# TensorE adds the gathered source rows in PSUM by identity products, in place of VectorE's addition

## The reference, cut to what matters

```python
h_src = h[row]
ef = jnp.concatenate([h_src, h[col]], axis=1)
edge_weights = jax.nn.sigmoid(jax.nn.relu(ef @ We1 + be1) @ We2 + be2)[:, 0]
aggr = jax.ops.segment_sum(edge_weights[:, None] * h_src, col, num_segments=n)
gate = jax.nn.sigmoid(jnp.concatenate([h, aggr], axis=-1) @ Wg + bg)
h_new = gate * aggr + (1.0 - gate) * h
```

## Time and profile before

| | us |
|---|---|
| median of 3 runs | 2142.13 (2141.02 to 2144.42) |
| span of the profiled execution | 2383.5 |

### The profile page before, as it was taken

One profiled execution on the slowest core, in us unless ns is written; L12 is line 12 of the kernel. 1 busy time (PEld: TensorE's weight loads), 2 busy tenths in 40 slices (PEclk: granted clock), 3 DMA queues, 4 the chain that ended last, 5 costly groups with the idle time before them and its releaser, 6 DMA issues.

```text
span 2383.5 us, 40155 instructions
## 1 busy us (share of the span) xinstructions
PE 1765.2 (74%) x12318; PEld 1600.5 (67%) x12319; DVE 1849.8 (78%) x5049; ACT 1086.9 (46%) x2658; POOL 1410.9 (59%) x1430
## 2 busy tenths in 40 slices
PE   4999986725654577878877878878877788777790
PEld 3787875525554576767777777777777787777760
DVE  7788777738986688887888877888887777777766
ACT  2566655635531244443444444454444433444325
POOL 4555303763666666666666666666666666666635
PEclk9999996966665567576667665666676656666665
DMA  7899991353444455545454555555555555555401
GB/s 274 293 331 327 332 305 41 118 179 91 124 121 135 118 154 145 152 145 157 144 154 146 155 152 162 161 163 153 154 165 163 160 155 161 162 159 156 141 24 54
DMA packets 278498, 392.59 MB, mean 165 GB/s; under 512 B 74753, under 2 KB 178436, under 8 KB 278155
## 3 DMA queue, kind: packets, MB, share of 16 engines
q1 hardware_dynamic: 218783, 230.00, 30.7%
q0 software_dynamic: 57024, 155.79, 22.1%
q10 hardware_dynamic: 2476, 4.22, 0.5%
HBM read 374.69 MB, written 15.12 MB: 164 GB/s over the span
## 4 chain that ended last, share of the span: by engine, by line
PE 59%; DVE 17%; issue 16%; DVEq 4%; another core or an unknown queue 3%; ACT 1%; DMA 0%; SPq 0%; POOL 0%; ACTq 0%; POOLq 0%
PE psum L585 13%; PE psum L535 8%; PE psum L1467 7%; PE psum L1468 7%; PE psum L1489 6%; PE psum L564 4%; DVE sums L1913 3%; PE psum L1497 3%; DVE weighted L580 3%; DVE psum L574 2%; PE psum L1446 2%; PE psum L1354 2%; DVEq L1978 2%; DVE logit L576 1%
## 5 line engine op out<-in xcount | busy, mean ns | idle before, releaser
L981 POOL DMA_INDIRECT x_rows<-src_table,lane_src x720 | 692.9, 962 | 397.6 <-issue 193.6
L574 DVE SCALAR_TENSOR_TENSOR psum<-psum,we_all 128x1024 f32<-128x1024 f32 (+1 forms) x273 | 268.9, 985 | 191.4 <-remote 116.6
L1468 PE MATMUL psum<-ring,sums 128*128 128x128 f32 x980 | 285.1, 372 | 99.0 <-issue 97.8
L589 DVE TENSOR_TENSOR sums<-sums,psum 128x128 f32 (+4 forms) x812 | 200.9, 247 | 189.7 <-issue 117.3
L1467 PE MATMUL psum<-ring,sums 128*128 128x128 f32 x980 | 294.1, 387 | 68.0 <-issue 65.6
L981 POOL DMA_INDIRECT late_gathers<-src_table,lane_src x232 | 224.5, 968 | 134.9 <-issue 61.9
L981 POOL DMA_INDIRECT ring<-src_table,lane_src x236 | 226.9, 962 | 123.0 <-issue 63.4
L1468 PEld LDWEIGHTS psum<-ring,sums 128*128 128x128 f32 x980 | 231.6, 282 | 99.0 <-issue 98.3
L576 DVE TENSOR_REDUCE logit<-psum 128x8 f32<-128x1024 f32 (+1 forms) x273 | 266.9, 978 | 21.9 <-issue 2.1
L585 PE MATMUL psum<-weighted,x_rows 128*128 128x40 f32 x1440 | 265.0, 359 | 23.2 <-issue 23.2
L585 PEld LDWEIGHTS psum<-weighted,x_rows 128*128 128x128 f32 x1440 | 264.1, 281 | 22.5 <-issue 22.5
(11 more groups left out here) (263 smaller groups left out, 3680.4 us busy)
## 6 DMA issues: line engine op xcount, KB each, us to landing
ring<-in_edge_attr SPq DMA_DIRECT2D x195, 512.0 KB, 5.3
ring<-rel_table SPq DMA_DIRECT2D x74, 512.0 KB
ring<-cell_table SPq DMA_DIRECT2D x121, 256.0 KB
ring<-src_table SPq DMA_DIRECT2D x144, 128.0 KB
x_rows<-src_table,lane_src POOLq DMA_INDIRECT x720
ring<-dst_table SPq DMA_DIRECT2D x297, 32.0 KB
ring<-src_table SPq DMA_DIRECT2D x104, 64.0 KB
src_table<-ring SPq DMA_DIRECT2D x12, 512.0 KB, 2.9
```

What stands on the lines that cost most here:

```text
L574: eng.scalar_tensor_tensor(hid, hid, 0.0, wide["we2"][:, :].unsqueeze(1).to_broadcast([P, n, P]), ALU.max, ALU.mult)
L589: return eng.tensor_tensor(table[..., bass.ds(start, width)], table[..., bass.ds(start, width)], part, ALU.add)
L981: eng.indirect_dma_start(gathered(c)[:, j, :], None, src_table, bass.IndirectOffsetOnAxis(ap=lane_src[:, t:t + 1], axis=0)).then_inc(gathe ...
L1468: last = eng.matmul(o, node_hot[:, u % 2, 1, e], base_dst[:, k % 2, :], start=False, stop=True, skip_group_check=True)
```

## The change

`add_src_part` becomes four TensorE products per chunk with the f32 identity as stationary operand and the gathered source part as moving operand. They accumulate onto the destination part: in `dst_part` only the first of four products starts a group, and the new ones end it. A new stage `hidden_sum(q)` stands last in TensorE's turn, behind `rider_mm`; it now has the wait for the gathers. VectorE waits for `hidden_sum` where it waited for `hidden` and the gathers, and its addition and the drain behind it are gone. The buffers, the other waits and all work on ScalarE, GpSimd and the DMA queues stay. In the setup one wait is written in another way (`step(last)`). The body of `far` treats edges out of reach of a chunk's window in the same way.

```diff
         def dst_part(eng, out, hot_t, win):
             for j in range(J):
-                last = eng.matmul(out[:, j, :], hot_t[:, j, :], win, start=True, stop=True, skip_group_check=True)
+                last = eng.matmul(out[:, j, :], hot_t[:, j, :], win, start=(j == 0), stop=False, skip_group_check=True)
             return last
 
         def add_src_part(eng, out, rows_):
-            return eng.tensor_tensor(out, out, rows_[:, :, 0:P], ALU.add)
+            for j in range(J):
+                last = eng.matmul(out[:, j, :], ident[:, :], rows_[:, j, 0:P], start=False, stop=True, skip_group_check=True)
+            return last
...
-            run_stages(n_steps, [(1, hidden_mm), (4, wsum), (1, rider_mm)])
+            def hidden_sum(q):
+                for j in range(2):
+                    eng.wait_ge(gather_in[q % (G_SLOTS // 2)][j], 32 * sum(len(pair_chunks(i)) for i in range(q % (G_SLOTS // 2), q + 1, G_SLOTS // 2)))
+                for c in pair_chunks(q):
+                    last = add_src_part(eng, hidden(c), gathered(c))
+                last.then_inc(done("hidden_sum"), 1)
+
+            run_stages(n_steps, [(1, hidden_mm), (4, wsum), (1, rider_mm), (1, hidden_sum)])
...
-                need(eng, "hidden", q)
-                for j in range(2):
-                    eng.wait_ge(gather_in[q % (G_SLOTS // 2)][j], 32 * sum(len(pair_chunks(i)) for i in range(q % (G_SLOTS // 2), q + 1, G_SLOTS // 2)))
+                need(eng, "hidden_sum", q)
                 n = len(pair_chunks(q))
-                add_src_part(eng, hidden_pair(q), gathered_pair(q))
                 need(eng, "weight", q - 4)
-                eng.drain()
                 edge_dots(eng, logit[:, q % 4, 0:n, :].rearrange("p c j -> p (c j)"), hidden_pair(q)).then_inc(done("logit"), 1)
```

More of the change, by code:

```diff
@@ L267, in gnn_pair @@
         assert own_slots % 2 == 0 and G_SLOTS % 2 == 0
[L269 to L280, removed]
         spare = ring_slots[RING_GATHERS]
@@ L1517, in far @@
                 eng.wait_ge(done("far_window"), item * 16)
-                dst_part(eng, hidden(0), onehot3_t[:, 0, 0, :, :], window[0:WP, 0, :]).then_inc(done("far_hidden"), 1)
+                dst_part(eng, hidden(0), onehot3_t[:, 0, 0, :, :], window[0:WP, 0, :])
+                eng.wait_ge(done("far_gather"), item * (16 * J))
+                add_src_part(eng, hidden(0), gathered(0)).then_inc(done("far_hidden"), 1)
                 eng.wait_ge(done("far_weigh"), item)
@@ L1562, in _ @@
                     last = eng.tensor_reduce(extent[0:n, g, k:k + 1], chunk_dst[0:n, g, :], AX.X, op)
-            last.then_inc(done("extent"), 1)
-            eng.wait_ge(done("extent"), 1)
+            step(last)
             eng.wait_ge(done("constants"), 1)
@@ L2020, in far @@
                 eng.wait_ge(done("far_hidden"), item)
-                eng.wait_ge(done("far_gather"), item * (16 * J))
-                add_src_part(eng, hidden(0), gathered(0))
-                eng.drain()
                 edge_dots(eng, logit[:, 0, 0, :], hidden(0)).then_inc(done("far_logit"), 1)
```

## The result

| | before | changed |
|---|---|---|
| median, us | 2141.77 (2141.02 to 2144.42, 4 runs) | 2087.43 (2085.86 to 2091.25, 4 runs) |
| profile after: run / span, us | | 2085.86 / 2084.1 |

The ratio is 0.9746 [0.9735, 0.9758]: 54 us less. The forecast was 20 us less and 2122; its low end of 2092 was 4.6 us too high. The direction and the mechanism held, the size did not.

A forecast was written before the change was run, and what follows sets the result against it. VectorE was taken to bind, GpSimd right behind; after the change gathers bind. 565.2 us, 1148 gathers at 1.255 or 1.268 us, and 109.2 us give 2115.1 or 2130.1; middle 2122, range 2092 to 2165.

The forecast's parts named there:

- What bounds the kernel now: Loop before the change: VectorE binds at a measured 10.23 us a step, GpSimd right behind at 10.04 to 10.14.
- The stalls are not in the runs of 2142 us: TensorE's matmul records 0.7 and 1.0 us apart belong to the profiled execution, 241 us longer than the runs' median.
- The pace of a gather: GpSimd in the loop: 0.95 us a gather and 0.30 before the next, 1.255 us undisturbed or 1.268 in the mean.
- The anchors of the sum: Fixed times around the last 1148 gathers: first waiting gather at 565.2 us, 109.2 us from the last one's end.
- 248 us of waits: GpSimd's 290 us of waits for released buffers, less 42 us of ordinary issue gaps; nearly the 241 us profile-to-runs difference.
- the two floors: Whole-kernel times at GpSimd's gather pace: 2115.1 us at 1.255 us a gather, 2130.1 at 1.268.
- What is removed: VectorE's chain loses 149 additions, 1.29 us each with drain, 191.6 us; 160 us of it off the path.
- What is added: TensorE gets 16 records a step, 1.8 us at full clock to 3.4 at half, hidden behind the gathers.
- What is moved: The wait for gathers goes from VectorE to the end of TensorE's next turn; hidden, with over 20 us left.
- GpSimd already binding: Rival, 17%: the loop already runs at gather pace, so removal shows only in the first and last steps; 2139 us.
- The quicker gathers: Rival, 10%: GpSimd's 0.305 us gaps between gathers are shorter outside the profile; 2050 to 2095 us.
- TensorE as the bound: Rival, 18%: new products run at clock 0.65, a step takes 10.6 us, +57 us, 2199; span 2150 to 2260.

The follow-up runs named there:

- Before with seven gathers: Kernel before with one of its eight gathers a step left out from the sixth step on: 2134.89 us, 0.9952; repeated 2132.54 us, 0.9954 (chip A).
- products and addition: Changed kernel with VectorE's addition and drain put back behind the eight products: 2145.62 us, 1.0015 on chip A; 2497.23 us, 1.0586 on chip B.
- second profile: Kernel before, unedited, run and profiled once more on chip A: median 2147.22 us, ratio 1.001; the profiled execution took 2149.8 us.
- change again: Changed kernel, unedited, run and profiled once more on chip A against the kernel before: 2093.01 us, 0.9764.
- before again: Kernel before, unedited, run and profiled once more on chip B: 2357.76 us, ratio 1.0.
- changed kernel with seven gathers: Changed kernel with one of eight gathers a step left out from the sixth step on: 1957.92 us, 0.9128; repeated 1951.32 us, 0.9117 (chip A).
- one product: Changed kernel with one identity product a step in place of eight: 2355.76 us, 0.9992 on chip B; 2086.93 us, 0.9733 on chip A.
- products twice: Changed kernel with its eight identity products issued twice a step: 2730.96 us, 1.1582 on chip B; 2092.11 us, 0.976 on chip A.

## Why the prediction was half right, step by step

**What bounds the kernel now: right for most of the loop.** Where sort rows are dense VectorE binds, with GpSimd's gathers 0.5 us a step behind (10.64 against 10.14). Before with seven gathers (0.9952) shows it from one side, products and addition (1.0015) from the other. In the last quarter, without sort rows, the gathers bind already. The prediction took one mean step, "its mean lies between", where there are phases; its own profile has 672 sort rows from 564 to 1850 us and none from there to 2275. The warning not to read the runs' bound from the 59% of TensorE in rows 1 was right; the chain of the second profile has it at 18%. The one step of VectorE on which I leaned was 10.95 us long and was said to run without a real wait, but it holds 0.43 us of idle time, in this row that rows 6 leave out:

```profile
1279.64 0.69 DVE L576 TENSOR_REDUCE logit<-psum 128x4 f32<-128x512 f32 x1 [0.43 <-issue]
```

In the second profile of before a step with sort rows is 10.49, without such a gap, start to start (VectorE's timeline):

```profile
1278.55 0.33 DVE L1913 TENSOR_SCALAR sums<-sums,src_low 128x128 bf16<-128x128 bf16 x1
...
1284.28 1.22 DVE L569 TENSOR_TENSOR psum<-psum,x_rows 128x1024 f32<-128x1024 f32 x1
...
1289.04 0.31 DVE L1913 TENSOR_SCALAR sums<-sums,src_low 128x128 bf16<-128x128 bf16 x1
```

**The stalls are not in the runs of 2142 us: right, for a reason that I had not thought of.** They are no effect of profiling: on chip B the same kernel has them and takes 2357 us each time, profiled or not. That the profile of rows 1 to 9 comes from such a chip is inferred from its rows. "A profiled execution of the changed kernel may well be longer" came from the same thought and did not happen, since that profile has no stalls.

**The pace of a gather: right.** 1.255 to 1.268 us forecast; in the second profile of before, in the changed kernel and in the change again the median from start to start is 1.251 to 1.254 and the mean, waits left out, 1.264 to 1.266.

**The anchors of the sum: wrong. This is the step that failed.** I found out that 241 us of the profile were not in the runs, and then read the 565.2 and the 109.2 off that same profile, as if all 241 lay between them. The 248 us of waits that agreed with the 241 made this look safe, and the agreement was chance: of the 235.6 us between that profile and the second one of before, (2274.3 - 565.2) - (2046.1 - 539.6) = 202.6 lie in the loop and 33 outside it. Nor is it true of the second profile that GpSimd "hardly waits": its 38 waits of 65.8 us are 54 us more than 38 gaps of 0.30 us, and that is the gain. The first gather that waits for a buffer, and the last one, in the second profile of before (GpSimd's timeline):

```profile
539.59 0.95 POOL L981 DMA_INDIRECT x_rows<-src_table,lane_src  x1 [10.84 <-PE psum L585]
...
2045.13 0.95 POOL L981 DMA_INDIRECT ring<-src_table,lane_src  x1 [0.30 <-issue]
```

in the changed kernel's first profile:

```profile
531.08 0.94 POOL L969 DMA_INDIRECT x_rows<-src_table,lane_src  x1 [4.81 <-PE psum L573]
...
1983.57 0.94 POOL L969 DMA_INDIRECT ring<-src_table,lane_src  x1 [0.30 <-issue]
```

and in that of the change again, taken on chip A beside the second profile of before:

```profile
537.51 0.94 POOL L969 DMA_INDIRECT x_rows<-src_table,lane_src  x1 [8.65 <-PE psum L573]
...
1988.17 0.95 POOL L969 DMA_INDIRECT ring<-src_table,lane_src  x1 [0.30 <-issue]
```

| us | profile of rows 1 to 9 | before again, chip B | before, second | change, first | change again |
|---|---|---|---|---|---|
| 41st gather, the first of the last 1148 | 565.2 | 558.1 | 539.6 | 531.1 | 537.5 |
| end of the last gather | 2274.3 | 2247.5 | 2046.1 | 1984.5 | 1989.1 |
| from there to the end | 109.2 | 109.1 | 101.8 | 99.6 | 102.0 |
| loop / 143.5 steps | 11.91 | 11.77 | 10.50 | 10.13 | 10.12 |

Head and tail together were taken at 674.4 us and are 641.4 in the second profile of before: 33 us too many. They did harm twice. The floor was 33 us too high: with 539.6 and 101.8 the two floors are 2082.1 and 2097.1 and their middle is 2089.6, 2 us from the 2087.43 measured. So close is in part luck, since the head alone differs by 6.4 us between the two profiles of the changed kernel. And since the median stayed what it was, the step of the kernel before came out too short, 10.23 where (2142.1 - 641.4) / 143.5 = 10.46 and the trace has 10.50, so that only 0.09 to 0.19 us a step seemed to be left to gain. It was 0.38 in the mean: of the 56.8 us between the two spans on chip A, 1506.5 - 1451.6 = 54.9 lie between the first waiting gather and the last one's end, 2.1 ahead of them, and nothing behind.

**What is removed: right in its size.** 149 additions, 1.29 us a step in VectorE's chain; in the mean 0.38 of them shows in the time and about 0.9 lie behind the gathers: 191.6 - 54.9 = 136.7 us are off the path where I had 160. With sort rows it is 0.5 and 0.8, and that those 0.8 are real is what the changed kernel with seven gathers shows (9.37 us a step against 10.14).

**What is added: right.** Sixteen records between 1.8 and 3.4 us, 1.86 in the median and 2.33 in the mean, at a clock that rose to 0.91. The Trainium skill (Perfetto Trace Analysis, "Identifying the Most-Contended Engine") judges TensorE's headroom by the busy share of weight loads, beside the share of its peak arithmetic. In the prediction the products brought that share from 71% to 100%, at 0.213 us a record. Measured, it is 1096.6 of 1416 us, 77%, with the products, and 1258.1 of 1416, 89%, with them doubled, and the time is the same in both. The traces agree that TensorE has headroom at these shares, but the 100% was made at the half clock's pitch: the share has to be read together with the granted clock, as the prediction allowed, and that went from 0.72 to 0.91 and 0.99.

**What is moved: right.** TensorE waits for gathers at L556 and VectorE behind it, 141.9 us, which costs nothing, since GpSimd waits for a buffer only 3.2 us.

**The rivals.** GpSimd already binding holds for the last quarter of the loop and not for most of the rest. Its argument had the sign wrong: it said that if part of the 241 us lies outside the loop, the loop of the runs is at the gathers' pace already. That part, 33 us, does lie outside, and it makes the loop of the runs longer, so that there is more to gain and not less. The quicker gathers and TensorE as the bound did not happen on chips A and C. The time of 2087 falls in the span that I gave to the quicker gathers (2050 to 2095), but not by their mechanism: the gaps are 0.30 us as before. TensorE as the bound is what chip B has, and already without the change. Rows 7 showed its stalls, and I priced them only as an addition to the rival. What the unedited change takes on chip B was not measured. From what stands around it, one product (2356) and products and addition (2497), it may well be slower than before there; that is a guess, and by how much stays open.

## What to carry to other kernels

When a profile's span is not the median of the runs, no time may be read off it as a place in the runs, neither a stage's start nor a tail's length; take durations and pitches of single instructions (those of the gathers and of VectorE's addition held here to 1%), and either profile again or let head and tail be a range in the sum (here 33 us wide, more than the forecast gain). Look whether the loop has phases before a mean step is used: here a quarter of it had nothing to gain. Work that moves from a binding engine to one with slack gains until the next engine's floor, and that floor is found by the pace of its own instructions (here 8 x 1.266 us of gathers), which one experiment with a gather less confirms on both kernels. A kernel that sits close to three engines' floors may have another bound on another chip, as the runs on chip B suggest, so time such a change on more than one.

## What the runs showed of the hardware

- The same program took 2142 us on chips A and C and 2357 on chip B, 10% apart, each repeatable within 0.6% (19 runs of the kernel before on chip B, in one sitting, and 41 on chips A and C). On chip B TensorE's matmul records come 0.6 us or more apart, two or more in a row and for 3.5 us in the median, in 78 of 143 steps of the gather loop ("before again"). What holds them there is not settled. The stretches end as a step's gathered packets run out: in "before again" the gathers' queue starts 43 packets in the last us of a stretch and 10 in the first us behind it, in "products twice" 54 and 31. That is an order in time and no cause; no run there changed the gathers.
- An indirect gather of 128 rows costs GpSimd 0.95 us and 0.30 us before the next, in every kernel and on both kinds of chip.
- An f32 product of 128 columns is two records, 0.213 us apart at the half clock and 0.110 to 0.116 at the full one. With sixteen more of them a step the granted clock of the loop on chip A went from 0.72 to 0.91, with thirty-two to 0.99, so that doubling them added 161 us of busy time in 1416 and 2.6 us to the median, within the spread of the runs.
